# Epilogue two scans later, exponentials one microsecond further ahead, in a Mamba-like layer

## What is computed

```python
xn = layernorm(x)                                  # x: 16 x 2048 x 1024
x_and_res = xn @ in_proj_w.T + in_proj_b
x_in, res = silu(x_and_res[..., :1024]), x_and_res[..., 1024:]
ssm = x_in @ x_proj_w.T + x_proj_b                 # 16 + 1024 + 1024 columns
dlt, Bm, Cm = ssm[..., :16], ssm[..., 16:1040], ssm[..., 1040:]
delta = clip(softplus(dlt @ dt_proj_w.T + dt_proj_b), 1e-5, 0.1)
# for each time step t, each of 1024 channels, each of 16 states:
h = clip(h * exp(A * delta) + Bm * delta * x_in, -100, 100)
y = sum_over_states(h) * Cm + D_param * x_in
out = x + (y * silu(res)) @ out_proj_w.T + out_proj_b + ffn(xn)
```

## Time and profile before

| what | value |
|---|---|
| time, median of 3 runs | 2258.88 us (2258.58 to 2259.79) |
| time of the profiled execution | 2262.19 us |
| its span, slowest core (core 2) | 2259.4 us |
| spans of the 8 cores | 2238.9 to 2259.4 us |
| VectorE busy | 1607.1 us (71%) |
| ScalarE busy | 1253.2 us (55%) |
| TensorE matmuls busy | 1246.1 us (55%) |
| GpSimd busy | 603.5 us (27%) |

### The profile page before, as it was taken

The page is one execution under the profiler, slowest core; times in us unless marked ns, Lnnn a source line. Parts: engine busy times, 40 slices in busy tenths (PEclk is TensorE's granted clock), DMA queues, the critical chain, the costliest instruction groups (busy, mean ns, idle before and its releaser), DMA issues.

```text
span 2259.4 us, 21671 instructions; the slowest of 8 cores (2238.9 to 2259.4 us)
## 1 busy us (share of the span) xinstructions
PE 1246.1 (55%) x5104; PEld 509.9 (23%) x5104; DVE 1607.1 (71%) x1600; ACT 1253.2 (55%) x1873; POOL 603.5 (27%) x506
## 2 busy tenths in 40 slices
PE   1222846156473857295729672867287637755444
PEld 1111313022031313141313231322132213222012
DVE  2322034059994999499949995899589967999980
ACT  0003464376556955586558655865587558745531
POOL 0000041317112071307131703171306131523001
PEclk9999966677585968597859775977588768866557
DMA  5672422621012400240033103310332022202001
GB/s 142 184 170 87 113 72 39 60 54 37 0 43 78 123 19 29 84 127 24 10 103 107 44 10 102 94 56 10 103 89 61 10 103 76 74 1 74 1 10 65
DMA packets 106881, 151.91 MB, mean 67 GB/s; under 512 B 53232, under 2 KB 53240, under 8 KB 106760
## 3 DMA queue, kind: packets, MB, share of 16 engines
q1 hardware_dynamic: 97128, 120.10, 18.6%
q0 software_dynamic: 6176, 19.93, 4.1%
q10 hardware_dynamic: 3456, 10.52, 1.5%
HBM read 124.26 MB, written 26.25 MB: 67 GB/s over the span
## 4 chain that ended last, share of the span: by engine, by line
PE 32%; DVE 24%; issue 13%; ACT 13%; DMA 9%; POOL 6%; SPq 1%; DVEq 0%; ACTq 0%; POOLq 0%
DVE h_buf L835 21%; PE pM L682 6%; PE pS L557 6%; DMA xr_t<-x 5%; PE pO L585 5%; PE pO L590 4%; ACT da L895 3%; PE pM L647 3%; POOL out_tm L473 3%; PE pO L682 3%; PE pO L647 2%; ACT rx L952 1%; ACT rx L948 1%; POOL wf L407 1%; PE pT L519 1%
## 5 line engine op out<-in xcount | busy, mean ns | idle before, releaser
L835 DVE TENSOR_TENSOR_SCAN h_buf<-da,cr,Bu 128x512 f16<-128x512 f16 x768 | 1048.8, 1424 | 116.9 <-PE pS L557 114.5
L895 ACT ACTIVATE da<-dlt,ac 128x512 f16<-128x512 f16 x1024 | 697.4, 715 | 359.6 <-DVE h_buf L835 358.7
L557 PE MATMUL pS<-h_buf,eye 128*128 128x512 f16 x1024 | 424.7, 474 | 339.0 <-DVE h_buf L835 329.1
L835 DVE TENSOR_TENSOR_SCAN h_buf<-da,Bu 128x512 f16<-128x512 f16 x256 | 334.5, 1365 | 156.3 <-ACT da L895 113.7
L454 POOL TENSOR_TENSOR Bu<-y_s,sres 128x512 f16<-128x512 f32 x64 | 124.9, 1951 | 754.9 <-DVE y_s L814 754.9
L557 PEld LDWEIGHTS pS<-h_buf,eye 128*128 128x128 f16 x1024 | 108.3, 107 | 587.1 <-issue 530.3
L682 PE MATMUL pM<-xin,rx 128*128 128x512 f16 (+1 forms) x832 | 196.3, 381 | 25.4 <-ACT sres L1020 17.7
L473 POOL TENSOR_TENSOR out_tm<-otm,xr_t 128x1024 f32<-128x1024 f16 x32 | 79.5, 2484 | 248.4 <-ACT otm L936 138.8
L585 PE MATMUL pO<-Bu,wo 128*128 128x512 f16 x512 | 134.1, 409 | 3.1 <-POOL Bu L454 3.1
L647 PE MATMUL pM<-xnf,rin 128*128 128x512 f16 x512 | 131.5, 405 | 2.4 <-ACT xnf L998 1.4
L647 PE MATMUL pO<-xnf,rin 128*128 128x512 f16 x512 | 124.5, 388 | 8.3 <-ACT da L895 5.7
(11 more groups left out here) (83 smaller groups left out, 1494.2 us busy)
## 6 DMA issues: line engine op xcount, KB each, us to landing
rin<-wt_in SPq DMA_DIRECT2D x128, 256.0 KB, 2.8
rx<-wt_x SPq DMA_DIRECT2D x128, 256.0 KB, 2.7
x_t<-x SPq DMA_DIRECT2D x32, 512.0 KB, 4.6
xr_t<-x POOLq DMA_DIRECT2D x32, 512.0 KB, 5.1
y<-out_tm SPq DMA_DIRECT2D x32, 512.0 KB, 3.6
wt_in<-rin SPq DMA_DIRECT2D x16, 256.0 KB, 3.0
wt_x<-rin SPq DMA_DIRECT2D x16, 224.0 KB, 3.7
x_t<-w_in ACTq DMA_DIRECT2D x4, 512.0 KB, 3.6
```

The source lines that it names most:

```text
L557: TCH(te.matmul(sbank[:, :], eye16[:, :], h_sl(gn), start=(n == 0), stop=(n == NST - 1)))
L835: s_n = VCH(v.tensor_tensor_scan(h_sl(gn), da_r[gn % DAR][:, :], Bu[P][k][:, :], init, op0=ALU.mult, op1=ALU.add))
L895: ACH(sc.activation(da_r[gn % DAR][:, :], dlt[Ps][k][:, :], AF.Exp, scale=c_(a_cols[k], n)))
```

## The change

Two constants. The epilogue of group `k-1` is emitted behind scan `n = 5` of group `k` and no longer behind `n = 3`; the last group's stays where it is. ScalarE's emission of exponentials looks 11.0 us ahead of the nominal time and no longer 10.0, in both forms of `apump()`.

```diff
-                        if n == 3 and k >= 1:
+                        if n == 5 and k >= 1:
                             if cS == 0 and k == 1:
                                 pass
                             elif cS == 0 and k == 2:
...
                     if block:
-                        B2 = bnd[min(ak[0] + 3, len(bnd) - 1)] + 10.0
+                        B2 = bnd[min(ak[0] + 3, len(bnd) - 1)] + 11.0
                     else:
-                        B2 = B + 10.0
+                        B2 = B + 11.0
```

## The result

The change makes the kernel faster. Its median over ten runs is 2242.7 us, that of the kernel before 2260.4 over ten runs beside it; the ratio is 0.9923 with a 95% interval of 0.9907 to 0.9940, or 17.4 us (14 to 21) of 2260.4. The forecast was a gain of 16.4 us and 2243 us. Some runs took over a per cent longer, at a lower granted clock on one die, and are left out of every ratio. The profiled execution has spans of 2219.6 to 2239.3 us on the eight cores, against 2238.9 to 2259.4.

The account below looks back on a forecast made before the run. VectorE's stream was taken as the bound, its idle time as what can be won. Chunk 0's 6.8 us plus 9.9 in chunks 1 to 6 less 0.3 gave 16.4 off 2258.88: 2242.5, predicted 2243, range 2237 to 2255.

Parts of the forecast that it names:

- The stall and the two scans: Chunks 1 to 6: scans 52 and 53 run inside L806's 7.7 us wait, winning 2.4 us per chunk.
- The hold of 0.55: Layernorm tile 3: the fourth short GpSimd operation is held to the end of scan 52, costing 0.55 us per chunk.
- s: Shift of the clock at which scan 51 ends in a chunk: -0.2 to +0.8 us, taken as +0.2.
- the first rival: Layernorm tile 3: both late GpSimd operations are held, 1.2 us more per chunk; 2251 us, chance 0.16.
- The look-ahead: 11.0 for 10.0: one exponential more ahead of layernorm tile 0, so tiles 0 to 2 come 0.6 us later.
- Chunks 1 to 6: Each chunk wins 2.4 - 0.55 - 0.2 = 1.6 us, six chunks 9.9.
- Chunk 0: ScalarE's chain ends 4.6 us earlier and two scans give 2.35, less 0.2 for a later stall end: 6.8 us.
- The cover of later exponentials: Scan 84's exponential is ready 4.9 us early, enough for 2.4 plus 1.45; 0.3 us set against other chunks, once.
- The slower rival: ScalarE's longer exponential blocks starve the scans, 2.6 us lost in each of six chunks: 2268 us, chance 0.06.
- Both held: Rival 1: both late GpSimd operations of layernorm tile 3 are held, a gain of 9 or 6 us; chance 0.16.
- no hold: Rival 2: tile 3's GpSimd operations pass between scans, so 14.2 + 6.8 = 21 us are won; chance 0.13.
- No change at all: Rival 3: the layernorm is late by all of 2.4 us and chunk 0's transfers end later: 2258 us, chance 0.10.

## Why the prediction was right

**The stall and the two scans.** Right: L806's wait fell from 7.7 to 5.8 us, and from L806 to the end of the chunk it is 2.6 us less (2.4 forecast).

**The hold of 0.55.** Right in kind and size, and shown from two sides. On the mean of chunks 1 to 6 scan 51 ends 0.22 us later in the chunk (s, forecast +0.2) and L806 starts 0.75 later, so the hold costs 0.53. In all 48 last tiles, of GpSimd's second to fourth operations, the fourth alone is held: it starts 0.49 us after the end of scan 51 and ends at 1.54 (forecast 0.5 and 1.57). With the layernorm off GpSimd the cost is gone. The 0.53 is a net figure. With the look-ahead alone, which takes one exponential away from ahead of tile 3, L806 comes 7.6 us after scan 51, for 8.0 before and 8.5 with the change; so the hold itself is 0.9, and 0.4 of it is paid by ScalarE. In the epilogue alone two operations are held, which is the first rival's mechanism: the second constant decides between the two. The margin is as small as the forecast said. The third operation starts 0.15 us after scan 51, where scan 52 starts at 0.28, and is free by 0.13; without the second constant it starts at 0.49 in five chunks of six and is held.

**The place of scan 51.** The mean of +0.22 is right in part by luck. By chunk, s is +0.9, +0.7, +0.1, -0.4, -0.2 and +0.2. For chunk 2 the forecast had -0.2, because the add of output tile 1 would run beside L806 for a part:

```profile
896.53 2.45 POOL L473 TENSOR_TENSOR out_tm<-otm,xr_t 128x1024 f32<-128x1024 f16 x1 [5.44 <-DMA xr_t<-x]
```

It took 2.45 us for 3.05 in the earlier trace rows. But its load came later: it started 54.2 us into the chunk and not 53.4, when L806 was over (896.14), and ended 0.2 later in the chunk than before. What moved the load stays open.

**The look-ahead.** Here the forecast's reading was incomplete. It charged +0.6 to s and named no gain for the edit, which so looked like a small loss. Alone it is one; with the epilogue it is worth 1.4 us per chunk, 8.5 in six, by the holds it spares. The forecast of both together was right because the one spared hold was in it (0.55 and not 1.75) and because the 0.9 behind the stall was nil with both edits and is only lost without the second. For that second part the forecast had no term, and that it came out at nil is luck.

**Chunks 1 to 6.** 1.8 us each for the forecast's 1.6, 10.9 for 9.9. The difference is 0.2 more behind the epilogue. The forecast's "230.4 us for 232" takes a length near that of five of the six chunks on core 2; chunk 4 is shorter (227.9), and the mean of the six there was 231.3.

**Chunk 0.** 6.8 us on the mean of cores for the forecast 6.8: 4.9 on ScalarE's chain (4.6), 2.8 behind L806 (2.35 of scans), less 0.9 for a later end of the long stretch (0.2). The mechanism is right; that the sum agrees to a tenth is luck, since three misses of 0.3 to 0.7 cancel. GpSimd's transfers took 75.8 us for 75.0 on the mean, and vary by 7 us from core to core in either kernel. On core 2 they took 78.0 us from the first issue to the gate product for 73.8, so it shows 3.3 only.

**The cover of later exponentials.** Right in kind: in chunk 2 exponential 84 is ready 1.7 us ahead of its scan, for 4.9 before, and in chunk 4, which has the least cover, scan 84 waits 0.65 us on core 2 (0.3 forecast) and less or nothing on the others. The view puts this wait down to TensorE; the exponentials are the later cause, since number 84 ends at 1449.1 and the scan starts at 1449.28. No other chunk waits there. The slower rival did not come about: VectorE waits 113.0 us for exponentials, of which 105.9 is the start, for 114.2 and 107.4.

**The other rivals.** Both held (2251) names what happens without the second constant, and no hold (2238) what happens without GpSimd in the layernorm; for this change both have the wrong count. No change at all is excluded.

What stays open is why GpSimd's operations cost VectorE 15.4 us of hold in its last 32 scans before, 15.0 with the change, 15.9 with the epilogue alone and 16.2 with the epilogue behind scan 7. That the time is hold is shown; that it depends on where a long GpSimd product falls against epilogues and scans was not tested by itself.

## What to carry to other kernels

Work moved into a stall is free only if it takes nothing from the chain that ends the stall: look at what that chain does in just those microseconds, and which port or engine it shares with the work moved in. Two constants changed together need a run apart as well as together, since here one alone wins 11 us, the other alone loses 5, and both win 17. Where the chain that ends the stall can be shortened itself (five GpSimd operations a tile replaced by four on ScalarE), that can be worth more than where the stalled engine's work is put: 40 us here against 17.

## What the runs showed of the hardware

In the kernel before, GpSimd's and VectorE's timelines at the start of the next delta products, in chunk 2 on core 2:

```profile
1022.70 1.40 POOL L483 TENSOR_SCALAR dlt<-dlt 128x512 f16<-128x512 f16 x1
1024.19 1.94 POOL L488 TENSOR_TENSOR Bu<-Bu,dlt 128x512 f16<-128x512 f16 x1
1026.09 1.15 POOL L491 TENSOR_TENSOR Bu<-Bu,dlt 128x512 f16<-128x512 f16 x1
```

```profile
1019.74 5.44 DVE L835 TENSOR_TENSOR_SCAN h_buf<-da,cr,Bu 128x512 f16<-128x512 f16 x4
1025.28 0.87 DVE L845 TENSOR_SCALAR cr<-h_buf 128x4 f16<-128x4 f16 x1
1026.07 0.68 DVE L806 TENSOR_TENSOR y_s<-pS,Cf 128x512 f32<-128x512 f32 x1
1026.85 0.93 DVE L814 SCALAR_TENSOR_TENSOR y_s<-xin,d_cols,y_s 128x512 f32<-128x512 f16 x1
```

The small copy L845 ends with the product L488 and takes 0.87 us, and 0.17 in a stretch without one; L806, which has one input in PSUM, takes 0.68 beside the product L491, as it does alone (0.69). L814, with two inputs in SBUF, starts 0.39 us before L491 ends and takes 0.93 for 0.75. It is the same over all cores in chunks 1 to 7, chunk 4 left out: 80 of L806's 336 instances run beside a GpSimd operation and take 0.68 us, the other 256 take 0.69; L814 takes 0.94 in 80 and 0.75 in 256. The Trainium skill (SBUF — State Buffer, Who interferes with whom) says that a VectorE instruction with at most one SBUF input, outside the two-port modes, stays out of the exclusion with GpSimd, one with two inputs does not, and a tensor-scalar operation can take the shared pair too. The three rows agree with it.

The other way round, a GpSimd operation on 128x1 takes 0.19 to 0.27 us alone and ends with the scan beside it otherwise, at up to 1.28 us. On VectorE's side the holds make 26 of the 196 us for which it counts as busy in a chunk: part of a busy engine's time is waiting. In the kernel before 8.0 of them lie beside gate products (L454), 5.6 beside output adds (L473) and 12 beside delta products (L480 to L500).

What I had not expected is the size of the effect of small shifts: one scan of delay of the epilogue, from 6 to 7, leaves VectorE with less idle time and costs 2.5 us of holds per chunk.
